# Two of 25 node groups take the sums of gathered rows of x over the edge blocks' own one-hots, instead of a count matrix

## The chip, the cores and the metric

One core of one Trainium2 chip runs the whole kernel. The metric is the device time of one execution in microseconds; the kernel before took 802.71 us (median of three runs, 802.51 to 804.0). TensorE is called PE, its weight loads PEld, VectorE DVE, ScalarE ACT, GpSimd POOL and SyncE SP.

## The reference

A graph layer over N = 6250 nodes and E = 206250 edges, sorted by `dst`, feature width 128, everything float32:

```
h = x @ W_node.T + b_node                  # [6250, 128]
e = edge_attr @ W_edge.T + b_edge          # [206250, 128]
msg = (h[src] + e) @ W_msg.T + b_msg
s = segment_sum(msg, dst, 6250);  deg = segment_sum(1, dst, 6250)
out = layernorm(x + s / max(deg, 1)[:, None])      # eps 1e-5, no scale or shift
```

All of it is linear before the norm. So the kernel needs, for each node, the sum of its edges' `edge_attr` rows and the sum of `x[src]` over its edges; both are multiplied by combined weights afterwards.

## The kernel before, in words

**Edge sums, by blocks.** The edges are cut into NS = 101 blocks of 2048 (16 tiles of 128 edges). A block's edges belong to some 64 neighbouring nodes. For each block SP loads the 1 MB of `edge_attr` into one of three slots of `edges` (`load_edges`); DVE makes 16 one-hots of 128 x 32 (`make_onehot`, L730) and one placing matrix (`make_place`, L736); PE sums the rows into four windows of 32 nodes (`sum_windows`, L547), ACT copies them (`copy_windows`, L1179), PE moves them to their place among 128 nodes (`place_windows`, L554) and DVE adds them into the column array `sums_e` at a column read from a register (`add_sums`, L746).

**Sums of x, by groups.** The nodes are cut into 25 groups of 250. A group takes one round. In it, for each pair of nodes, one window of 125 edge sources is fetched by an indirect DMA on POOL's queue (`load_window`, L479, three rounds ahead); DVE turns the sources into a block number and a row number (`make_keys`) and into one-hots of both (`make_hots`, L756: `row_hot` and `key_hot`, one pair of instructions for 25 windows, five pairs a round); PE multiplies them into counts (`count_fill`, L615, 125 matmuls a round, five to a fill, 25 fills a round), ACT moves each bank of counts to SBUF (`move_bank`, L1235), and in the next round PE multiplies all of x, split into three bfloat16 parts, with the counts (`apply_counts`, L630, 147 matmuls of 250 columns spread over the fills). The result, `x[src]` summed for 250 nodes, is copied to `group_x` (`take_x`), and `finish_group` (L641, L642) multiplies both sums with the weights; DVE and ACT make residual and norm, SP stores.

**Order.** The order is written out by hand, the same on every engine: 8 leading slots with one block each, then rounds of five slots s = 0 to 4, each slot of five fills. Edge blocks come in pairs, nearly always at the start of slots s = 2 and s = 4 of a round (`blocks_at`); the finish of an earlier group is in slot s = 0. PE works strictly in this order: it sums a slot's blocks, then does the fills; the blocks are placed after the slot's second fill. DVE makes the one-hots of slot g + 1 first in slot g, then does the adds of that slot's blocks. The blocks start at number 27 and wrap around, since the first 7 groups are done last. POOL's queue holds only the fetching of windows after some 110 us. SP's queue holds the edge loads in block order, with residual loads and stores between them.

If one of several checks on the inputs (sortedness, how far the edges of the groups reach) fails, a slow general path runs; every limit of those checks is met by these inputs with room, before and after the change.

## Time and profile before

| | before |
|---|---|
| median of 3 runs | 802.71 us |
| profiled execution, its own time | 799.62 us |
| span of its trace | 797.7 us |
| PE busy | 716.8 us (90%) |
| PEld busy | 649.6 us (81%) |
| DVE busy | 640.0 us (80%) |
| ACT busy | 467.9 us (59%) |
| POOL busy | 84.3 us (11%) |
| mean DMA rate | 152 GB/s |
| mean granted clock of PE | 0.987 of full speed |

The span is what the trace covers; the execution's own time is 1.9 us longer. Busy times are sums of the instructions' durations with overlaps counted once, so they tell how full an engine is, and the idle places have to be looked for in the slices, the chain and the timelines.

### The profile page before, as it was taken

The page shows a single profiled execution, that of the slowest core. Times are in us where ns is not written, and L with a number is a line of the kernel's source. Part 1 is how long each engine was busy: PE and PEld are TensorE (multiplying, and loading weights), DVE is VectorE, ACT ScalarE, POOL GpSimd, SP SyncE. Part 2 cuts the span into 40 slices and gives each one's busy share as a digit, 9 for nine tenths or more (in the row PEclk, how much of TensorE's full clock was granted, in tenths as well). Part 3 has the DMA queues.
Part 4 walks back from the last instruction along what each step waited for, and adds up shares of the span by engine and source line. Part 5 has one row for each costly group of instructions (what it writes and reads, how often), then busy time and mean ns, then how long its engine had stood idle before and what let it go on. Part 6 is the DMA issues. An engine that isn't in the chain of part 4 may idle for free.

```text
span 797.7 us, 24927 instructions
## 1 busy us (share of the span) xinstructions
PE 716.8 (90%) x10573; PEld 649.6 (81%) x10573; DVE 640.0 (80%) x1137; ACT 467.9 (59%) x948; POOL 84.3 (11%) x63
## 2 busy tenths in 40 slices
PE   2634458999999999999999999999999999999995
PEld 2523347899899999899999999998999999999995
DVE  7508998799988888888888888888888888888832
ACT  4103955576566666666666666566656666666641
POOL 2113734001000000000000000000000000000000
PEclk9999979999999999999999999999999999999999
DMA  6985334363365436243645463453345543644000
GB/s 209 209 268 176 106 108 128 108 229 123 130 207 173 169 118 236 59 170 119 228 135 182 144 227 125 155 186 117 123 149 187 186 160 118 221 150 174 31 14 16
DMA packets 71806, 121.11 MB, mean 152 GB/s; under 512 B 4717, under 2 KB 17738, under 8 KB 71591
## 3 DMA queue, kind: packets, MB, share of 16 engines
q1 hardware_dynamic: 68462, 115.72, 43.5%
q0 software_dynamic: 2496, 2.84, 1.5%
q8 instruction: 87, 1.43, 0.8%
q10 hardware_dynamic: 734, 0.90, 0.5%
q14 instruction: 27, 0.22, 0.1%
HBM read 116.19 MB, written 3.23 MB: 150 GB/s over the span
## 4 chain that ended last, share of the span: by engine, by line
PE 75%; DVE 14%; issue 4%; DMA 4%; SPq 2%; DVEq 1%; ACT 0%; ACTq 0%
PE x_ps L630 44%; PE count_ps L615 15%; PE win_ps L547 10%; DVE key_hot L756 3%; DVE row_hot L756 3%; PE win_ps L554 3%; DMA edges<-in_edge_attr_dram 2%; SPq L394 2%; DVE onehot L730 1%; PE misc_ps L641 1%; PE misc_ps L642 1%; DVE dve_junk L851 1%; DVE place L736 1%; DMA region<-in_dst_dram 1%; DMA rows_words<-starts_dram 1%
## 5 line engine op out<-in xcount | busy, mean ns | idle before, releaser
L1235 ACT CAST region<-count_ps 128x490 bf16<-128x490 f32 x625 | 354.1, 574 | 186.8 <-PE count_ps L615 182.2
L630 PE MATMUL x_ps<-region,x_rest 128*128 128x250 bf16 x2450 | 448.4, 269 | 0.0
L630 PE MATMUL x_ps<-region,x_hi 128*128 128x250 bf16 x1225 | 332.0, 271 | 0.5 <-ACT region L1235 0.5
L615 PE MATMUL count_ps<-key_hot,row_hot 125*128 125x98 bf16 x3125 | 242.4, 209 | 27.4 <-DVE key_hot L756 17.5
L756 DVE TENSOR_TENSOR row_hot<-iota_bf,row 125x3200 bf16<-125x3200 bf16 x125 | 229.8, 1838 | 34.2 <-PE count_ps L615 32.2
L630 PEld LDWEIGHTS x_ps<-region,x_rest 128*128 128x128 bf16 x2450 | 229.3, 98 | 17.2
L615 PEld LDWEIGHTS count_ps<-key_hot,row_hot 125*128 125x128 bf16 x3125 | 201.3, 98 | 50.0 <-DVE key_hot L756 20.6
L756 DVE TENSOR_TENSOR key_hot<-iota_bf,key 125x2500 bf16<-125x2500 bf16 x125 | 183.4, 1467 | 0.0
L547 PE MATMUL win_ps<-edges,onehot 128*32 128x128 f32 x3232 | 108.7, 290 | 18.7 <-DMA edges<-in_edge_attr_dram 16.9
L630 PEld LDWEIGHTS x_ps<-region,x_hi 128*128 128x128 bf16 x1225 | 118.7, 97 | 8.3 <-ACT region L1235 0.6
L547 PEld LDWEIGHTS win_ps<-edges,onehot 128*32 128x32 f32 x3232 | 91.4, 116 | 31.4 <-issue 29.8
L479 POOL DMA_INDIRECT win_src<-in_src_dram,clipped_int x25 | 47.8, 1910 | 528.1 <-DVE key_bf L785 406.6
L1179 ACT COPY win_sb<-win_ps 128x128 f32<-128x128 f32 x101 | 26.7, 267 | 95.2 <-PE win_ps L547 90.8
L746 DVE TENSOR_TENSOR sums_e<-sums_e,win_ps 128x128 f32 x101 | 29.1, 288 | 58.6 <-DVE sums_e L746 23.6
L730 DVE TENSOR_TENSOR onehot<-iota_bf,rel_col 128x512 f32<-128x512 bf16 x101 | 68.4, 715 | 0.0
L554 PE MATMUL win_ps<-place,win_sb 128*128 128x128 f32 x202 | 35.4, 297 | 6.4 <-DVE place L736 4.1
L554 PEld LDWEIGHTS win_ps<-place,win_sb 128*128 128x128 f32 x202 | 29.0, 204 | 9.2 <-ACT win_sb L1179 4.5
L736 DVE TENSOR_SCALAR place<-iota_f,pos 128x128 f32<-128x128 f32 x101 | 30.4, 339 | 0.0
L1253 ACT ACTIVATE y<-y,shift,rstd 125x128 f32<-125x128 f32 x50 | 21.9, 487 | 1.9 <-DVE shift L824 1.9
L795 DVE SCALAR_TENSOR_TENSOR y<-misc_ps,recip,resid 125x128 f32<-125x128 f32 x50 | 15.1, 344 | 8.9 <-PE misc_ps L642 8.9
L1242 ACT COPY group_x<-x_ps 128x250 f32<-128x250 f32 x25 | 9.2, 369 | 18.2 <-PE x_ps L630 16.5
L641 PE MATMUL misc_ps<-w_both,sums_e 128*125 128x128 f32 x100 | 19.2, 274 | 0.5 <-issue 0.5
(166 smaller groups left out, 341.9 us busy)
## 6 DMA issues: line engine op xcount, KB each, us to landing
edges<-in_edge_attr_dram SPq DMA_DIRECT2D x101, 1024.0 KB, 7.1
resid<-in_x_dram SPq DMA_DIRECT2D x25, 125.0 KB
out_dram<-y SPq DMA_DIRECT2D x25, 125.0 KB
region<-in_dst_dram ACTq DMA_DIRECT2D x1, 768.0 KB
win_src<-in_src_dram,clipped_int POOLq DMA_INDIRECT x25, 7.5
region<-in_L_gnn_W_node_dram SPq DMA_DIRECT2D x1, 64.0 KB
region<-in_L_gnn_W_edge_dram SPq DMA_DIRECT2D x1, 64.0 KB
region<-in_L_gnn_W_msg_dram SPq DMA_DIRECT2D x1, 64.0 KB
```

Of the source, the lines that this page charges most:

```text
L479: pool.indirect_dma_start(out=win_src[:, m % 3, :], out_offset=None, in_=src.rearrange("(r e) -> r e", e=WE), in_offset=bass.IndirectOffse ...
L547: mm = pe.matmul(bank[q * W:(q + 1) * W, 0:D], hot[:, q * J + j, :], edges[:, t % EDGE_SLOTS, q * J + j, :], start=(j == 0), stop=(j == J ...
L554: pe.matmul(l2_ps[t % 2], win_sb[:, t % 2, :], place[:, t % 2, :], start=True, stop=True).then_inc(l2_done, 1)
L615: mm = pe.matmul(count_ps[fill % COUNT_BANKS][:, k * KEYS:(k + 1) * KEYS], row_hot[0:WE, g % 2, f * FILL + k, :], key_hot[0:WE, g % 2, f * ...
L630: mm = pe.matmul(x_ps[m % 2][:, 0:NB], rows, counts[m % 2][:, b, :], start=(n == 0), stop=(n == PARTS - 1))
L641: pe.matmul(to, sums_e[:, first + h * PB:first + (h + 1) * PB], w_both[:, 1, :], start=True, stop=False)
L730: dve.tensor_tensor(onehot[:, t % ONEHOT_SLOTS, :, :], iota_bf[:, 0:W].rearrange("p (a w) -> p a w", a=1).to_broadcast([P, TILES, W]), rel ...
L736: dve.tensor_scalar(place[:, t % 2, :], iota_f[:, :], pos[:, sup_of[t]:sup_of[t] + 1], None, ALU.is_equal).then_inc(place_ready, 1)
L746: dve.tensor_tensor(to, to, l2_ps[t % 2], ALU.add).then_inc(added, 1)
L756: ins = dve.tensor_tensor(hot[0:WE, g % 2, :, :].rearrange("p w (a b) -> p w a b", b=4), iota_bf[0:WE, 0:width].rearrange("p (c a b) -> p ...
L1179: act.copy(win_sb[:, t % 2, :], win_ps[t % 2][:, 0:D]).then_inc(win_copied, 1)
L1235: act.copy(counts[m % 2][:, :, f * FILL * 2:(f + 1) * FILL * 2], count_ps[fill % COUNT_BANKS][:, 0:FILL * KEYS].rearrange("p (n b) -> p b ...
```

## The change

Groups 0 and 1 (nodes 0 to 499) no longer get a round: the rounds go from 25 to 23, and so do windows, keys, hots, counts and their application. For nine edge blocks (blocks 0 to 8, which cover nodes 0 to some 560) the rows `x[src]` are gathered from DRAM: 16 indirect DMAs of 128 rows of 512 B each on POOL's queue, into a new buffer `x_gathered` (one buffer, 1 MB in all). PE then runs `sum_windows` and `place_windows` a second time for that block, as a second *item*, with the same one-hots and the same placing matrix and `x_gathered` in the place of the edge rows; DVE adds the result into 700 other columns of `sums_e`, which ACT sets to zero before. `finish_group` takes the sum of x for groups 0 and 1 from there.

The nine blocks are taken in slot s = 3 of rounds 5, 6, 8, 10, 12, 13, 15, 17 and 19, a slot that had no block before: in it PE sums the edge rows first and the gathered rows next. The other 92 blocks keep the pairs in slots 2 and 4. The 16 gathers of a block are all asked for when PE has filled bank 25r - 7 of the counts (in slot 3 of the round before, r being the block's round), so 22 fills before slot 3 of round r. The first of them also waits until the block before has used `x_gathered`. The numbers of the sources come by nine direct DMAs on SP's queue (16 bytes a piece), early on. The two extra finishes lie in slot 3 of rounds 14 and 20.

```diff
+GX = 2
+XBLOCKS = 9
-    ROUNDS = GROUPS
+    ROUNDS = GROUPS - GX
...
+    XSEG = 3
+    x_round = [5 + 14 * k // (XBLOCKS - 1) for k in range(XBLOCKS)]
+    x_slot = [LEAD + SEGS * m + XSEG for m in x_round]
...
+    x_fill = []
+    for k in range(XBLOCKS):
+        room = (x_round[k] - x_round[k - 1] if k > 0 else 2) * ROUND_FILLS
+        x_fill.append([x_round[k] * ROUND_FILLS + XSEG * FILLS - room + 2 + (room - 24) for i in range(TILES)])
+    pool_loads = sorted([(ROUND_FILLS * (m - 3) + 10, 0, m) for m in range(2, ROUNDS)] + [(x_fill[k][i], 1, k * TILES + i) for k in range(XBLOCKS) for i in range(TILES)])
...
+                if LEAD <= t < LEAD + XBLOCKS:
+                    k = t - LEAD
+                    with nc.allow_non_contiguous_dma(reason="four sources a piece"):
+                        sp.dma_start(x_index[:, k, :].rearrange("p (q j) -> p q j", q=Q),
+                                     src[k * SUP:(k + 1) * SUP].rearrange("(q p j) -> p q j", q=Q, j=J)).then_inc(x_index_in, 16)
...
-            for m in range(2, ROUNDS):
-                load_window(m)
+            def load_rows(k, i):
+                if i == 0:
+                    pool.wait_ge(x_index_in, 16 * XBLOCKS)
+                    pool.wait_ge(src_index_ready, 3)
+                    if k > 0:
+                        pool.wait_ge(l1_done, last_item[sup_of.index(k - 1)] + 1)
+                pool.wait_ge(bank_filled, x_fill[k][i])
+                pass_waits()
+                pool.indirect_dma_start(out=x_gathered[:, i, :], out_offset=None, in_=x[:, :],
+                                        in_offset=bass.IndirectOffsetOnAxis(ap=x_index[:, k, i:i + 1], axis=0)).then_inc(rows_in, 16)
+
+            for fill, kind, at in pool_loads:
+                if kind == 0:
+                    load_window(at)
+                else:
+                    load_rows(at // TILES, at % TILES)
...
-            def sum_windows(t):
-                hot, bank = onehot[:, t % ONEHOT_SLOTS, :, :], win_ps[t % 2]
+            def sum_windows(v):
+                t, k = item_of[v]
+                hot, bank = onehot[:, t % ONEHOT_SLOTS, :, :], win_ps[v % 2]
                 pe.wait_ge(onehot_ready, t + 1)
...
-                pe.wait_ge(edge_in[t % EDGE_SLOTS], 16 * (t // EDGE_SLOTS + 1))
+                if k is None:
+                    pe.wait_ge(edge_in[t % EDGE_SLOTS], 16 * (t // EDGE_SLOTS + 1))
+                else:
+                    pe.wait_ge(rows_in, 16 * TILES * (k + 1))
...
+                        rows = edges[:, t % EDGE_SLOTS, q * J + j, :] if k is None else x_gathered[:, q * J + j, :]
...
+                if u == ZERO_X:
+                    act.wait_ge(fin_mm, ZERO_FIN)
+                    act.copy(sums_e[:, X_COLS:X_COLS + X_LONG], zero_col[:, 0:1].to_broadcast([P, X_LONG])).then_inc(zeroed, 1)
```

On DVE three small instructions are new ahead of the rounds (`base_x`, `limit_x` and a check). The scratch of the early node counting moves into `x_gathered`.

## Rows read from the trace of the kernel before

**Rows 1.** The page, part 1: busy us of each engine, its share, instructions.
```profile
PE 716.8 (90%) x10573; PEld 649.6 (81%) x10573; DVE 640.0 (80%) x1137; ACT 467.9 (59%) x948; POOL 84.3 (11%) x63
```

**Rows 2.** The chain in order of time: start us, us, what (two of its pairs).
```profile
431.38 1.88 PE win_ps L547 x64
...
458.61 1.88 PE win_ps L547 x64
```

**Rows 3.** PE's timeline: start us, us, engine, line, operation, count.
```profile
438.00 0.38 PE L615 MATMUL count_ps<-key_hot,row_hot 125*128 125x98 bf16 x5
...
439.62 0.39 PE L615 MATMUL count_ps<-key_hot,row_hot 125*128 125x98 bf16 x5
...
445.95 0.52 PEld L554 LDWEIGHTS win_ps<-place,win_sb 128*128 128x128 f32 x4
...
446.39 0.35 PEld L615 LDWEIGHTS count_ps<-key_hot,row_hot 125*128 125x128 bf16 x5
...
452.36 0.29 PEld L641 LDWEIGHTS misc_ps<-w_both,sums_e 128*125 128x125 f32 x2
...
453.24 0.34 PEld L615 LDWEIGHTS count_ps<-key_hot,row_hot 125*128 125x128 bf16 x5
```

**Rows 4.** POOL's timeline: the indirect DMAs of L479, five of 25.
```profile
57.43 1.21 POOL L479 DMA_INDIRECT win_src<-in_src_dram,clipped_int  x1 [27.56 <-DVEq L881]
58.95 1.21 POOL L479 DMA_INDIRECT win_src<-in_src_dram,clipped_int  x1 [0.30 <-issue]
...
124.43 2.82 POOL L479 DMA_INDIRECT win_src<-in_src_dram,clipped_int  x1 [0.30 <-issue]
127.56 2.80 POOL L479 DMA_INDIRECT win_src<-in_src_dram,clipped_int  x1 [0.30 <-issue]
...
433.91 1.90 POOL L479 DMA_INDIRECT win_src<-in_src_dram,clipped_int  x1 [25.34 <-DVE key_bf L785]
```

**Rows 5.** DVE's timeline beside two of these.
```profile
124.35 1.83 DVE L756 TENSOR_TENSOR row_hot<-iota_bf,row 125x3200 bf16<-125x3200 bf16 x1
...
432.91 1.82 DVE L756 TENSOR_TENSOR row_hot<-iota_bf,row 125x3200 bf16<-125x3200 bf16 x1
```

**Rows 6.** DVE's timeline over one round, its long instructions that matter.
```profile
439.64 1.82 DVE L756 TENSOR_TENSOR row_hot<-iota_bf,row 125x3200 bf16<-125x3200 bf16 x1
...
442.75 1.82 DVE L756 TENSOR_TENSOR row_hot<-iota_bf,row 125x3200 bf16<-125x3200 bf16 x1
...
448.01 1.28 DVE L730 TENSOR_TENSOR onehot<-iota_bf,rel_col 128x512 f32<-128x512 bf16 x2
449.22 1.82 DVE L756 TENSOR_TENSOR row_hot<-iota_bf,row 125x3200 bf16<-125x3200 bf16 x1
...
453.77 1.83 DVE L756 TENSOR_TENSOR row_hot<-iota_bf,row 125x3200 bf16<-125x3200 bf16 x1 [1.36 <-PE count_ps L615]
...
460.14 1.82 DVE L756 TENSOR_TENSOR row_hot<-iota_bf,row 125x3200 bf16<-125x3200 bf16 x1
...
465.70 1.29 DVE L730 TENSOR_TENSOR onehot<-iota_bf,rel_col 128x512 f32<-128x512 bf16 x2
466.91 1.82 DVE L756 TENSOR_TENSOR row_hot<-iota_bf,row 125x3200 bf16<-125x3200 bf16 x1
```

**Rows 7.** The answer on line 479: time from issue to landing of its DMAs.
```profile
DMA to landing us min/median/max: 3.3/7.5/9.3
```

**Rows 8.** The page, part 6: KB each, median us from issue to landing.
```profile
edges<-in_edge_attr_dram SPq DMA_DIRECT2D x101, 1024.0 KB, 7.1
```

**Rows 9.** Stretches: length, PE, PEld, DVE, ACT, POOL busy, granted clock, DMA.
```profile
400.00:500.00 100.00, 100.00 (x1567) 91.61 (x1565) 86.81 (x144) 64.15 (x130) 7.59 (x4) 1.00 0.49 163
...
130.00:140.00 10.00, 6.85 (x78) 6.09 (x76) 8.11 (x22) 3.33 (x6) 2.26 (x2) 0.92 0.59 203
140.00:150.00 10.00, 9.59 (x149) 8.12 (x148) 6.61 (x13) 5.67 (x12) 0.00 (x0) 0.91 0.46 144
```

**Rows 10.** The chain in order of time around that stretch.
```profile
132.46 5.02 DMA rows_words<-starts_dram
```

More of the change, by code:

```diff
@@ L95, in gnn_layer @@
-    summed_by = [blocks_by[u] for u in finish_slot]
-    assert not any(blocks_at[u] for u in finish_at)
-    LIMIT_B = (39.5, 3.7)
-    LIMIT_A = (6.0, 3.7)
-    for m, done in enumerate(summed_by):
-        if m < B_ROUNDS:
-            assert LIMIT_B[0] + LIMIT_B[1] * m <= FIRST + done or FIRST + done >= NS, m
-        else:
-            assert done == NS or LIMIT_A[0] + LIMIT_A[1] * (m - B_ROUNDS) <= FIRST + done - NS, m
+        due = u + 1 if u < LEAD else min(NS - XBLOCKS, LEAD + 2 * pairs)
@@ new lines, in gnn_layer @@
+        blocks_at.append(list(range(len(sup_of), len(sup_of) + due - ordered_by[-1])))
+        sup_of += ordered[ordered_by[-1]:due]
+        item_of += [(t, None) for t in blocks_at[u]]
+        ordered_by.append(due)
+        if u in x_slot:
+            assert not blocks_at[u]
+            k = x_slot.index(u)
+            blocks_at[u].append(len(sup_of))
+            item_of += [(len(sup_of), None), (len(sup_of), k)]
+            sup_of.append(k)
+        items_by.append(len(item_of))
+    ITEMS = len(item_of)
@@ new lines, in gnn_layer @@
+    finishes = [(LEAD + SEGS * (m + 2) if m < ROUNDS - 2 else SLOTS, m, None) for m in range(ROUNDS)]
+    for i in range(GX):
+        u = x_slot[X_DONE[i] - 1] + SEGS
+        finishes.append((u if u not in x_slot else u + SEGS, None, i))
+    finishes.sort(key=lambda f: f[0])
+    finish_slot = [f[0] for f in finishes]
+    finish_of = {m: n for n, (u, m, i) in enumerate(finishes) if m is not None}
+    finished = [i if m is None else group_of[m] for u, m, i in finishes]
+    finish_at = {u: n for n, u in enumerate(finish_slot) if u < SLOTS}
@@ new lines, in gnn_layer @@
+    assert not any(blocks_at[u] for u in finish_at) and len(finish_at) == GROUPS - 2
+    ZERO_FIN = 1 + max(n for n, g in enumerate(finished) if g * NB < X_COLS + X_LONG and (g + 1) * NB > X_COLS)
+    ZERO_X = finish_slot[ZERO_FIN - 1] + 1
+    assert ZERO_X < x_slot[0] and X_COLS >= N0 + P and (GX - 1) * NB + 322 + P <= X_LONG
+    LIMIT_B = (39.5, 3.7)
+    LIMIT_A = (5.3, 4.0)
+    LIMIT_X = (3.0, 2.0)
+    for u, m, i in finishes:
+        done = FIRST + ordered_by[u]
+        if m is None:
+            assert LIMIT_X[0] + LIMIT_X[1] * (2 * i + 1) <= X_DONE[i]
+        elif m < B_ROUNDS:
+            assert LIMIT_B[0] + LIMIT_B[1] * m <= done or done >= NS, m
+        else:
+            assert done == NS + FIRST - XBLOCKS or LIMIT_A[0] + LIMIT_A[1] * group_of[m] <= done - NS + XBLOCKS, (m, done)
@@ L159, in gnn_layer @@
         before_hot = [words.rearrange("p (j n) -> p j n", j=TILES) for words in before_words]
[L160 to L161 removed]
+        act_junk = [spare[:, k * JUNK:(k + 1) * JUNK].bitcast(BF16) for k in range(2)]
+        dve_junk = [spare[:, (2 + k) * JUNK:(3 + k) * JUNK].bitcast(BF16) for k in range(2)]
         is_last = sb("is_last", [P, 1])
@@ L634, in finish_group @@
             def finish_group(n):
-                first = group_of[n] * NB
-                pe.wait_ge(added, summed_by[n])
-                pe.wait_ge(x_taken, n + 1)
+                u, m, i = finishes[n]
+                first = finished[n] * NB
+                pe.wait_ge(added, items_by[u])
+                if m is not None:
+                    pe.wait_ge(x_taken, m + 1)
+                    x_sums = group_x[:, m % 2, :]
+                else:
+                    x_sums = sums_e[:, X_COLS + i * NB:X_COLS + (i + 1) * NB]
                 free_misc()
```

137 lines of the change are left out of this document (78 added, 59 removed).

## The prediction

> **What bounds the kernel now.** Read first the engines' shares: PE is busy for 90% of the span and DVE for 80%, POOL for 11% [rows 1]. Then the stretches: between 400 and 500 us PE is busy for 100.00 of 100 us at full clock, DVE for 86.81 [rows 9]. So in the steady part PE's own instruction stream sets the pace, DVE has 13 us in 100 to spare, and what PE does not have to execute is gained in full, as long as nothing makes it wait. The chain shows the period: the block pair of slot 2 starts at 431.38 in one round and at 458.61 in the next [rows 2], so a round takes 27.23 us.
>
> **What is removed.** A pair of blocks costs PE 1.88 us for the sums [rows 2] and 446.39 - 445.95 = 0.44 us for the placing [rows 3], together 2.32. A finish costs 453.24 - 452.36 = 0.88 us [rows 3]. Both are done as often as before (101 blocks, 25 finishes), only in fewer rounds. What a round costs beyond them is 27.23 - 2 x 2.32 - 0.88 = 21.71 us, and two such rounds go: **-43.4 us**. DVE loses two rounds of one-hots too, so it does not become the bound: it keeps about its share.
>
> **What is added on PE.** Nine more items at half a pair's price: 9 x 1.16 = **+10.4 us**, if the rows are there. The half pairs in slot 3 make one slot as full as the pair slots around it; DVE prepares one block's one-hots for it instead of two's, so I take nothing for it.
>
> **Whether the gathered rows are there.** This decides the case. One round of before serves as the clock. The slot s = 3 begins with the fill at 438.00, its third fill is at 439.62 and over at about 440.0 [rows 3]; that is bank 25r - 7, at which POOL may begin. The rows are needed one round after the slot's start, at 438.00 + 27.23 = 465.23, plus 0.94 for the edge item that goes first: 466.17. The budget is 26.2 us for 16 gathers and the landing of the last.
>
> What a gather costs is not in the trace, but its nearest row is close: the window fetch, the same instruction with 125 rows of 500 B for 128 of 512 B. Alone it takes 1.21 us, and the next begins 58.95 - 57.43 = 1.52 after it [rows 4]. Beside DVE it is longer: 2.82 us where it began just after a `row_hot` (124.43 after 124.35), and the next one began 3.13 later and took 2.80. At 433.91 it took 1.90 and ended at 435.81; the `row_hot` beside it ran from 432.91 to 434.73 [rows 4, 5]. Both cases fit one rule: a gather that begins under a `row_hot` ends 1.08 us after the `row_hot` does (434.73 + 1.08 = 435.81; 124.35 + 1.83 + 1.08 = 127.26, seen 127.25). The `key_hot` that follows at once didn't hold it. I take that each gather needs a moment, about 0.1 us after its start, in which no `row_hot`, `key_hot` or `onehot` runs, and 1.09 us from there, with 0.30 between two.
>
> By this I walk through the round [rows 6], with the ends of `row_hot` at 441.46, 444.57, 451.04, 455.60 and 461.96. The gathers end at 442.6, 445.7, 447.2, 448.7, 450.4 (behind the `onehot` that ends at 449.29), 452.1, 453.6, 456.7, 458.2, 459.8, 463.1, 464.6 and 466.1. Thirteen are out when PE arrives. By then DVE has one more pair of hots in hand (466.91 to 470.1), after which it stops, as its adds need PE. The last three end at 468.1, 469.8 and 471.3. The last one starts at 470.1, and no edge load is under way by then, so I add the least landing time of 3.3 [rows 7]: 473.4, a stall of 7.2 us. With one gather more slipped in between two instructions it is 5.7. I take **7.0 us, nine times: +63.0**. Least: no hold by DVE at all, 440.1 + 15 x 1.52 + 3.3 = 466.2, a stall of 0.0. Most: the last lands at the median of 7.5 instead of 3.3 and one more gather is held for a `row_hot`, 7.2 + 4.2 + 1.6 = 13. PE is the bound and all five slots of a round are full, so nothing makes the stall good later. Behind PE's waiting instruction stand the placing, the fills and the counts of x; DVE waits in its adds for the placing, ACT for banks. In round 17 the pair of slot 2 is missing, which makes the budget 2.3 shorter; that is within the 7.0's error.
>
> The Trainium skill speaks of this place: *SBUF — State Buffer*, section "Who interferes with whom", has the port pair that DVE and GpSimd share as an exclusive lock, but lets `tensor_tensor` take only its read interface and infers that descriptor generation, which writes, isn't held up by it. By that rule the gathers would run at the pace of the undisturbed ones and the stall would vanish. The trace doesn't agree: beside a TENSOR_TENSOR the same instruction took 1.90 and 2.82 instead of 1.21 us.
>
> **The clock after a stall.** Once before, PE stood for 5.02 us on a DMA (132.46) [rows 10]. The granted clock is 0.92 in the stretch 130 to 140 and 0.91 in 140 to 150 [rows 9], with PE at work again from 137.5. A fall from 2.4 to 1.2 GHz counts half, so that is 10 x 0.17 x 2 = 3.4 us at the lower level, 1.7 us lost. A stall of 7 us should cost the same each time: 9 x 1.7 = **+15.3 us**. Least 0, most twice that.
>
> **Small parts.** Three small instructions on DVE before the rounds, where the chain runs through DVE: +0.5 us at a guess, bounds 0 and 1. The zeroing of 700 columns is ACT's, which is 59% busy [rows 1]: 0. The nine index loads go through SP's queue ahead of edge loads; an edge load takes 7.1 us to land [rows 8] and is asked for three blocks ahead, so one moved by some 1 to 2 us is still in time: 0, at most 9 x 1 = 9 if the early part has no such cover. The gathers move 9 x 1 MB more over DMA engines that were half used (0.49 in the steady stretch [rows 9]): 0.
>
> **The sum.** 797.7 - 43.4 + 10.4 + 63.0 + 15.3 + 0.5 = 843.5 us of span. The profiled execution's own time is 1.9 above its span (799.62), and the median of the runs is 3.1 above that: **848.5, say 848 us**, 5.7% slower. The likeliest case's own range is 825 to 880: stalls of 5.7 to 9.5 us with 0 to 2.5 for the clock.
>
> **The rivals.**
> *The gathers are in time* (the side of faster). Mechanism: POOL's instruction gets its moment at every change of instruction on DVE, or the source of the hold is something that gathers with ready indices don't need. Then stall and clock cost are gone: 797.7 - 43.4 + 10.4 + 0.5 + 5.0 = 770 us. For it: 1.21 us and a period of 1.52 undisturbed; the sum fits the budget to 0.0. Against: all steady fetches took 1.90. The point from which it decides is (43.4 - 10.4 - 0.5) / 9 = 3.6 us per block, clock included. Chance 0.14. By the rule of the Trainium skill weighed above (*SBUF — State Buffer*, "Who interferes with whom") this is what happens.
> *A short stall*, 0.5 to 3.5 us per block and hardly a fall of the clock: 775 to 801, at its middle 788. For it: DVE's pattern beside new slots may leave more room than in my walk. Chance 0.08.
> *A long stall.* The landing is at the median or worse since the gathers share the engines with edge loads asked for at the same time, and a `key_hot` holds a gather too: 13 us and 2.5 of clock per block, 770 + 9 x 15.5 = 909; half way to it 880 to 900. For it: 7.5 is the median landing time. Against: during the stall hardly an edge load is asked for. Chance 0.12.
> *The change doesn't do what it says*: an input check fails and the general path runs, at many times 800 us. The limits and the node counts leave room; chance under 0.01.
>
> The main case has 0.65. The range for 8 in 10 takes in the short stall's upper part and most of the long one: 782 to 888. A difference under 0.2% (1.6 us) can't be told from none here: faster 0.22, the same 0.01, slower 0.77.
>
> **What would show it.** In the changed trace: a period of 27.2 us in rounds without a gathered block; nine waits of PE's `win_ps` for a DMA into `x_gathered`, 5 to 9 us each, and these rounds at 27.2 + 1.2 + 7 + 1.7 = 37 us; POOL's gathers at 1.2, 1.9 and 2.8 us by where they start, some 13 before PE arrives; the granted clock under 1.00 behind each wait. The prediction is wrong if the waits are under 3.6 us, and the mechanism is wrong if the gathers' durations don't go with DVE's `row_hot`.

## The result and the profile after

| | before | after |
|---|---|---|
| median, four runs each on the same chip | 802.61 us | 926.87 us |
| ratio, with its interval | | 1.1547 (1.151 to 1.1584) |
| span of the trace | 797.7 us | 925.6 us |
| mean granted clock of PE | 0.987 | 0.906 |

The change costs 15.5% where 5.7% was forecast; the time lies above the range's 888. All medians below are of runs beside a kernel before on the same chip, which took 800.2 to 802.6 us; each kernel was run twice, but e3 ten times, e9 five, e13 and e17 four. The ratios are of fast executions: one of e13's four, with 2423.57 us, and one of the kernel before beside it, with 875.22, are left out, and no trace shows what slowed them.

The page after, part 1 and PE's share and clock in 40 slices; the first line answers to [rows 1]:

```profile
PE 749.2 (81%) x10331; PEld 641.0 (69%) x10331; DVE 609.9 (66%) x1120; ACT 438.7 (47%) x902; POOL 249.0 (27%) x205
...
PE   3444489999896997997895978993998897799996
...
POOL 2123620011826027008207061035008208100000
```

PE executes 242 matmuls fewer than before in 128 us more. Its share falls in single slices, most of them slices in which POOL's digit is high. The stretch that answers to [rows 9] (us, then busy us and number of instructions of each engine, PE's clock, DMA share, GB/s) has PE busy for 85.44 us where it was 100.00:

```profile
400.00:500.00 100.00, 85.44 (x1173) 70.97 (x1171) 64.17 (x104) 46.27 (x94) 36.73 (x29) 0.89 0.41 133
```

The forecast wanted nine waits of PE for a DMA into `x_gathered`. The trace has none. This is the answer on the tile `x_gathered` for PE after (288 matmuls form the 144 of x's second items twice over, since a float32 matmul is shown as two); under "idle before it" stands nothing:

```profile
L622 PE MATMUL win_ps<-x_gathered,onehot x288: 272/273/273, 267.8 to 805.4; 128*32 128x128 f32 x144
its engine sat idle before it (us, times) until:
who waited for it (us, times):
```

Besides waits for PE itself, what stands long in the waits after is "issue", an engine that waited for nothing that the trace shows, and "remote", an event without a known sender (engine, tile and line, what ended the idle time, us in total, times, longest):

```profile
ACT region L1327 <- remote: 87.8, 23, 10.8
DVE row_hot L841 <- remote: 86.1, 8, 15.7
...
PEld win_ps L622 <- issue: 57.5, 87, 17.6
PEld x_ps L705 <- issue: 49.1, 42, 14.6
```

So the lost time begins at PE. POOL's timeline shows the first burst (start us, us, engine, line, operation, idle before); it answers to [rows 4]:

```profile
228.26 5.87 POOL L565 DMA_INDIRECT x_gathered<-in_x_dram,x_index  x1 [32.10 <-PE count_ps L690]
234.44 0.95 POOL L565 DMA_INDIRECT x_gathered<-in_x_dram,x_index  x1 [0.30 <-PE count_ps L690]
...
237.22 2.03 POOL L565 DMA_INDIRECT x_gathered<-in_x_dram,x_index  x1 [0.30 <-issue]
239.56 1.06 POOL L565 DMA_INDIRECT x_gathered<-in_x_dram,x_index  x1 [0.30 <-issue]
...
243.43 1.60 POOL L565 DMA_INDIRECT x_gathered<-in_x_dram,x_index  x1 [0.30 <-issue]
...
246.70 0.94 POOL L565 DMA_INDIRECT x_gathered<-in_x_dram,x_index  x1 [0.30 <-issue]
247.95 0.94 POOL L565 DMA_INDIRECT x_gathered<-in_x_dram,x_index  x1 [0.30 <-issue]
...
254.19 0.94 POOL L565 DMA_INDIRECT x_gathered<-in_x_dram,x_index  x1 [0.30 <-issue]
```

And PE in the same time, in three stretches:

```profile
236.00:246.00 10.00, 9.24 (x111) 8.26 (x108) 7.42 (x8) 5.31 (x10) 8.17 (x7) 1.00 0.43 149
247.00:258.00 11.00, 6.16 (x26) 1.81 (x26) 1.74 (x10) 1.14 (x2) 7.52 (x8) 0.62 0.21 52
259.00:266.00 7.00, 7.00 (x86) 5.99 (x79) 4.09 (x9) 2.97 (x8) 0.00 (x0) 0.69 0.54 170
```

In the middle stretch PE executes 26 matmuls in 11 us, 2.4 a us, against 11 before it and 12 behind it. Its timeline there (the sums of an ordinary pair of edge blocks, whose rows and one-hots are long there) has small groups with gaps between them:

```profile
247.20 0.86 PE L622 MATMUL win_ps<-edges,onehot 128*32 128x128 f32 x4
248.39 0.38 PE L622 MATMUL win_ps<-edges,onehot 128*32 128x128 f32 x3 [0.33 <-issue]
249.83 0.44 PE L622 MATMUL win_ps<-edges,onehot 128*32 128x128 f32 x2 [1.06 <-issue]
250.56 0.37 PE L622 MATMUL win_ps<-edges,onehot 128*32 128x128 f32 x1 [0.29 <-issue]
```

I call this crawling. It begins while gathers go out back to back, lasts until some 3 us after the last one's instruction (over at 255.13 in this block, PE back at its rate at 258.5), and occurs in all nine blocks, in pair sums as here or in the fills. The clock follows: 1.00 in the first stretch, 0.62 in the second, where the trace has 2.4 GHz until 249.7 and 1.2 GHz for the 13.7 us from there. Of stretches of 2 us, 72 after 200 us hold fewer than 24 instructions of PE (matmuls and weight loads) where 50 are usual; before, none does until its last 10 us. They hold 675 instructions, worth 27 us at 50 to 2 us, so 144 - 27 = 117 us are lost in them.

The other engines also hear from PE late, and this makes "issue" and "remote" less empty than they look. ACT moves one bank of counts for each fill, in order, so its n-th cast belongs to the n-th fill. In the seventh block two fills end at 624.75 and 625.61, and their banks are moved at 632.05 and 641.23, though ACT had nothing else to do:

```profile
624.36 0.39 PE L690 MATMUL count_ps<-key_hot,row_hot 125*128 125x98 bf16 x5
...
625.22 0.39 PE L690 MATMUL count_ps<-key_hot,row_hot 125*128 125x98 bf16 x5
...
632.05 0.57 ACT L1327 CAST region<-count_ps 128x490 bf16<-128x490 f32 x1 [5.18 <-remote]
641.23 0.57 ACT L1327 CAST region<-count_ps 128x490 bf16<-128x490 f32 x1 [8.60 <-remote]
...
641.86 0.39 PE L705 MATMUL x_ps<-region,x_hi 128*128 128x250 bf16 x1 [13.94 <-issue]
```

The trace's record of the semaphore that PE counts up for the second of these fills stands at 641.21, 15.6 us after the fill. PE's next instruction needs all banks of its round moved and starts 0.06 us after the cast is over, so these 13.94 us of "issue" are a wait for ACT, which itself waited for PE's late word (540 records of ACT's own semaphore are in the trace for 575 casts, against 574 in e1's). Counted over the fills after 200 us, ACT starts more than 0.5 us behind both the fill and its own work before in 49 of 481 cases, up to 10.8 us and 125.6 us in all; in the kernel before it never starts more than 0.04 us behind.

The length of the rounds says where (us between ACT's copies of the row numbers, one a round, worked out from the traces; after, and e1, which is after without gathers):

```
after  35.8 38.5 30.6 27.5 28.8 43.9 43.0 27.2 45.5 27.2 44.9 25.4 51.7 51.3 27.2 50.4 27.2 42.7 27.2 45.8 27.2 29.5
e1     35.8 38.6 28.8 27.5 28.9 30.9 28.3 27.2 30.8 27.2 30.8 25.4 30.8 30.8 27.2 33.0 27.2 27.2 27.2 30.8 27.2 29.5
```

Rounds of the steady part without gathers take 27.2 us, as [rows 2] has it; rounds in which a block is gathered take 13 to 21 us more than the same rounds of e1.

### The profile page after: what moved, and what is told of

It is laid out like the page before. It is cut to its first block, busy times and chain, and to the rows that moved or that the text cites. A ratio compares the mean times of both kernels' runs of the same rounds, so it can differ in the third digit from the quotient of the medians.

```text
span 925.6 us, 24735 instructions
## 1 busy us (share of the span) xinstructions
PE 749.2 (81%) x10331; PEld 641.0 (69%) x10331; DVE 609.9 (66%) x1120; ACT 438.7 (47%) x902; POOL 249.0 (27%) x205
## 4 chain that ended last, share of the span: by engine, by line
PE 59%; DVE 16%; issue 11%; another core or an unknown queue 6%; DMA 3%; SPq 1%; ACT 1%; DVEq 1%; ACTq 0%
PE x_ps L705 32%; PE count_ps L690 12%; PE win_ps L622 11%; DVE key_hot L841 4%; DVE row_hot L841 4%; PE win_ps L629 2%; DMA edges<-in_edge_attr_dram 2%; DVE onehot L811 1%; SPq L444 1%; PE misc_ps L721 1%; PE misc_ps L722 1%; DVE x_gathered L936 1%; DVEq L822 1%; ACT region L1327 1%
## 5 line engine op out<-in xcount | busy, mean ns | idle before, releaser
L1327 ACT CAST region<-count_ps 128x490 bf16<-128x490 f32 x575 | 323.4, 574 | 294.8 <-PE count_ps L690 200.5
L705 PE MATMUL x_ps<-region,x_rest 128*128 128x250 bf16 x2254 | 434.6, 278 | 12.7 <-issue 12.3
L705 PE MATMUL x_ps<-region,x_hi 128*128 128x250 bf16 x1127 | 315.5, 280 | 25.5 <-issue 22.1
L841 DVE TENSOR_TENSOR row_hot<-iota_bf,row 125x3200 bf16<-125x3200 bf16 x115 | 211.6, 1840 | 131.5 <-remote 86.1
L565 POOL DMA_INDIRECT x_gathered<-in_x_dram,x_index x144 | 177.3, 1231 | 344.2 <-PE count_ps L690 306.1
L690 PEld LDWEIGHTS count_ps<-key_hot,row_hot 125*128 125x128 bf16 x2875 | 190.7, 101 | 83.6 <-issue 38.3
L705 PEld LDWEIGHTS x_ps<-region,x_rest 128*128 128x128 bf16 x2254 | 216.9, 101 | 40.8 <-issue 21.5
L841 DVE TENSOR_TENSOR key_hot<-iota_bf,key 125x2500 bf16<-125x2500 bf16 x115 | 168.6, 1466 | 0.0
L622 PE MATMUL win_ps<-edges,onehot 128*32 128x128 f32 x3232 | 128.9, 298 | 39.8 <-DMA edges<-in_edge_attr_dram 17.3
L534 POOL DMA_INDIRECT win_src<-in_src_dram,clipped_int x23 | 35.3, 1535 | 156.1 <-issue 77.6
L629 PEld LDWEIGHTS win_ps<-place,win_sb 128*128 128x128 f32 x220 | 32.2, 206 | 19.6 <-issue 13.7
```

The lines of the kernel that those rows point to most:

```text
L534: pool.indirect_dma_start(out=win_src[:, m % 3, :], out_offset=None, in_=src.rearrange("(r e) -> r e", e=WE), in_offset=bass.IndirectOffse ...
L565: pool.indirect_dma_start(out=x_gathered[:, i, :], out_offset=None, in_=x[:, :], in_offset=bass.IndirectOffsetOnAxis(ap=x_index[:, k, i:i ...
L622: mm = pe.matmul(bank[q * W:(q + 1) * W, 0:D], hot[:, q * J + j, :], rows, start=(j == 0), stop=(j == J - 1))
L629: pe.matmul(l2_ps[v % 2], win_sb[:, v % 2, :], place[:, t % 2, :], start=True, stop=True).then_inc(l2_done, 1)
L690: mm = pe.matmul(count_ps[fill % COUNT_BANKS][:, k * KEYS:(k + 1) * KEYS], row_hot[0:WE, g % 2, f * FILL + k, :], key_hot[0:WE, g % 2, f * ...
L705: mm = pe.matmul(x_ps[m % 2][:, 0:NB], rows, counts[m % 2][:, b, :], start=(n == 0), stop=(n == PARTS - 1))
```

## The experiments

All kernels are the changed kernel with the edit shown. The first question: is the loss in a wait for the rows, in the gathers themselves, or in the rest?

**e1, no gathers.**

```diff
-                pool.wait_ge(bank_filled, x_fill[k][i])
-                pass_waits()
-                pool.indirect_dma_start(out=x_gathered[:, i, :], ...).then_inc(rows_in, 16)
+                if k == 0 and i == 0:
+                    pool.memset(x_gathered[:, :, :], 0.0).then_inc(rows_in, 16)
```

> The 144 gathers are left out; POOL sets the buffer to zero once, and PE doesn't wait for rows. It leaves out the sums of x for groups 0 and 1. Everything else of the change stays: 23 rounds, nine second items, index loads. Both theories: the terms -43.4 and +10.4 of my sum hold, and the time is 770 us (765 to 776), all of the loss belongs to the gathers. If it is over 790, the loss lies in the new order of blocks or in the second items.

Measured: 780.1 us, ratio 0.9751 (0.9724 to 0.9779). Everything but the gathers is a gain, if a smaller one than my 32.5 us of span: 797.7 - 779.6 = 18.1. A part of the missing 14.4 is a wait that I had priced at nothing, PE for DVE's one-hots in the slot behind the extra one:

```profile
PE win_ps L618 <- DVE onehot L807: 8.4, 8, 1.1
```

Of the other 6 us, 2.4 lie ahead of the first copy of row numbers (68.7 us against 66.3) and 1.6 behind the last (59.6 against 58.0); the rest is not located. The gathers cost 926.9 - 780.1 = 147 us, 16.3 a block.

**e2, the same bursts, and nothing waits for them.** The second items sum edge rows again, and POOL alone keeps count of the gathers; the output for 500 nodes is thus other than the reference's.

```diff
-                    sp.wait_ge(l1_done, first_item[t - EDGE_SLOTS] + 1)
+                    sp.wait_ge(l1_done, last_item[t - EDGE_SLOTS] + 1)
...
+                        pool.wait_ge(rows_in, 16 * TILES * k)
...
-                    pe.wait_ge(rows_in, 16 * TILES * (k + 1))
+                    pe.wait_ge(edge_in[t % EDGE_SLOTS], 16 * (t // EDGE_SLOTS + 1))
```

> All gathers run as in the changed kernel, in the same bursts, but the second items sum the edge rows again, so that nothing waits for the gathered rows; it leaves out the sums of x for groups 0 and 1. Theory A (the burst itself slows PE's instructions, whoever waits for it): as slow as the changed kernel, 927 us (915 to 935), PE at some 5 instructions per us in the bursts. Rival W (PE is late because its rows land late, and the slow matmuls are how the trace shows this wait): 770 us (765 to 780).

Measured: 924.6 us, 1.1558 (1.1521 to 1.1595), as with the waits. The wait that my forecast was built on is worth nothing here; PE crawls all the same.

**e3, gathers spread.** One every 2 to 3 fills instead of all at once.

```diff
-        x_fill.append([x_round[k] * ROUND_FILLS + XSEG * FILLS - room + 2 + (room - 24) for i in range(TILES)])
+        x_fill.append([x_round[k] * ROUND_FILLS + XSEG * FILLS - room + 2 + i * (room - 5) // TILES for i in range(TILES)])
```

> The 16 gathers of a block are spread evenly over all fills since the block before (45 of 50 fills for seven blocks, one gather in 2.8 fills, 20 of 25 fills for two blocks, one in 1.25 fills). Theory A, with a backlog that builds up only when gathers follow each other at 1.25 us: seven blocks lose nothing, two lose some; 770 + 2 x 0 to 17 us, that is 770 to 805, likeliest 785. If the damage goes with the number of gathers and not with their rate: 927 as before. Rival W: rows are asked for earlier, 770 to 780.

Measured: 802.8 us, 1.0031 (1.0015 to 1.0048), all of the output computed. The same 144 gathers, and 124 of the 147 us are gone. What is left is mostly in the two blocks that have only one round between them and the block before, whose 16 gathers stand 1.25 fills apart: 37.6 and 39.7 us instead of 28.3 and 30.8 of e1, together 18 of 23 us.

**e4, a quarter of the bytes, and e5, a quarter of the rows.** Both fill only a part of the buffer, which is zero elsewhere.

```diff
-                pool.indirect_dma_start(out=x_gathered[:, i, :], out_offset=None, in_=x[:, :],
+                pool.indirect_dma_start(out=x_gathered[:, i, 0:32], out_offset=None, in_=x.rearrange("n (h e) -> (n h) e", e=32),
```

```diff
-                pool.indirect_dma_start(out=x_gathered[:, i, :], out_offset=None, in_=x[:, :],
-                                        in_offset=bass.IndirectOffsetOnAxis(ap=x_index[:, k, i:i + 1], axis=0)).then_inc(rows_in, 16)
+                pool.indirect_dma_start(out=x_gathered[0:32, i, :], out_offset=None, in_=x[:, :],
+                                        in_offset=bass.IndirectOffsetOnAxis(ap=x_index[0:32, k, i:i + 1], axis=0)).then_inc(rows_in, 16)
```

> As the changed kernel in number and time of the gathers, but each fetches 128 pieces of 128 B instead of 128 rows of 512 B (wrong rows, the rest of the buffer zero). Theory A by descriptors, semaphore writes or POOL's generation: 927 us stays (over 900). Theory A by bytes moved: under 810 us. Rival W: somewhat faster landing, 880 to 927.

> As the changed kernel, 16 gathers in a burst per block, but each fetches 32 rows instead of 128 (the rest of the buffer stays zero, so the sums of x for groups 0 and 1 lack three quarters of their rows). Descriptors and bytes go to a quarter, the number of DMAs and of their completions stays. Theory A1 (the number of descriptors, or POOL's time on them): the slow stretches vanish, 780 to 795 us. Theory A2 (the completions, one per DMA engine and gather): 900 us or more stays, as the burst even gets denser.

Measured: 921.2 us (1.1515, 1.149 to 1.154) and 936.5 us (1.168, 1.157 to 1.179). Fewer bytes or fewer rows make it no better. Most gathers of 32 rows took 0.87 us, those of 128 rows 0.94: what an indirect DMA costs on POOL is nearly all fixed.

**e6 and e7, other paces.** Groups of four gathers every 11 fills (5 in the two narrow blocks), and one gather every 1.5 fills (1.25 there).

```diff
+        ... - room + 2 + i // 4 * (5 if room == 25 else 11) for i in range(TILES)])     # e6
+        ... - room + (2 + i * 20 // TILES if room == 25 else 20 + i * 3 // 2) for i in range(TILES)])     # e7
```

> Gathers in groups of four back to back, a group every 11 fills (seven blocks) or every 5 fills (two blocks, the mean rate of the two dense blocks in the run with even spreading). If it takes a backlog of six or more gathers at 1.25 us to slow PE: no slow stretch in the seven blocks, and hardly one in the two: 785 to 795 us. If every gather that follows another at 1.25 us costs: 840 us or more.

> In seven blocks a gather every 1.5 fills (1.6 us) instead of every 2.8; the two dense blocks at 1.25 fills as with even spreading, where they cost some 9 us each. If the limit lies between 1.25 and 1.5 us a gather: 800 to 806 us, like even spreading. If at 1.6 us the backlog builds up too: 830 to 870.

Measured: 828.0 us, 1.0327 (1.025 to 1.040), and 818.6 us, 1.021 (1.013 to 1.029). The wide rounds lose some 0.5 to 5 us each; single gathers, though closer together on average than the groups, cost less than groups of four.

**e8, the same pieces by SP.** 16 direct DMAs of 128 rows by SP's hardware queue in place of POOL's, of rows in their natural order (so the sums of x for 500 nodes are of other rows, as in e10, e11 and e15).

```diff
+                while asked < XBLOCKS and slot_of[t] >= x_slot[asked] - 4:
...
+                    for i in range(TILES):
+                        sp.dma_start(x_gathered[:, i, :], x[i * P:(i + 1) * P, :]).then_inc(rows_in, 16)
```

> No gathers; SP asks for 16 direct DMAs of 128 rows of 512 B each per block, in a run, some four slots ahead: same number of DMAs, of 512 B pieces, of bytes and of completions into the same semaphore, but by SP's hardware queue (rows 0 to 2047 of x each time, so the sums of x for groups 0 and 1 are wrong ones). If any such burst slows PE: over 850 us. If it takes POOL's software-made descriptors: 780 to 800 us, less 0 to 10 of edge loads that come later.

Measured: 790.5 us, 0.9859 (0.9815 to 0.9904). No crawling; 10 us above e1, of which one round took 41.9 instead of 30.8 for an edge load that came late behind them. The landing of 9 MB more, its writes to SBUF and its semaphore updates are thus harmless to PE's stream, and the fault is with POOL's part.

The second question: what about POOL's instruction is it?

**e10 and e11, direct DMAs by POOL,** 16 of 128 rows or one of 2048:

```diff
-                pool.indirect_dma_start(...)
+                pool.dma_start(x_gathered[:, i, :], x[i * P:(i + 1) * P, :]).then_inc(rows_in, 16)     # e10
+                pool.dma_start(x_gathered[:, :, :], x[0:TILES * P, :].rearrange("(i p) d -> p i d", p=P)).then_inc(rows_in, 16)     # e11, i == 0 only
```

> The changed kernel with each indirect gather replaced by a plain direct DMA of POOL, of 128 rows of 512 B with known addresses (the sums of x for 500 nodes are then of other rows), 16 in a burst at the same place, the same bytes and the same completion. If it is the indirection (reading the indices, one descriptor a row computed from them) that slows PE, this stands with the gathers left out or with SP's sixteen direct DMAs: 780 to 795. If it is any burst of DMAs whose descriptors POOL makes, PE crawls here too: 900 to 930. Between them if direct descriptors are made in less time.

> As the sixteen direct DMAs of POOL, with one direct DMA of 2048 rows of 512 B in their place; rows are thus other ones again. If the number of POOL's DMA instructions decides: 780 to 790. If the descriptors it makes decide: as the sixteen direct ones. If direct ones of POOL are harmless altogether, both stand at 780 to 795 and the fault is with the indirect form.

Measured: 779.4 us, 0.9729 (0.9695 to 0.9763), and 777.2 us, 0.9701 (0.9669 to 0.9733). Harmless; but 16 of them are through in some 9 us, which is shorter than the 19 us after which PE began to crawl in the first block (in the fifth and sixth, on the sums of a pair, 3 us were enough, and e10 shows nothing there either). **e15** makes the stretch as long, with 48 direct ones of 48, 48 and 32 rows, and **e16** keeps POOL busy as long without any DMA (16 memsets of the buffer; the sums of x of 500 nodes are zero):

```diff
+                for a, b in ((0, 48), (48, 96), (96, 128)):
+                    pool.dma_start(x_gathered[a:b, i, :], x[i * P + a:i * P + b, :]).then_inc(rows_in, 16)     # e15
+                if k * TILES + i > 0:
+                    pool.wait_ge(rows_in, 16 * (k * TILES + i))
+                pool.memset(x_gathered[:, :, :], 0.0).then_inc(rows_in, 16)     # e16
```

> As the sixteen direct DMAs of POOL (e10, 779.4 us, a burst of some 8.7 us), with 48 direct ones of 48, 48 and 32 rows in their place, some 0.55 us each, so a burst of about 25 us, as long as that of the 16 gathers (rows of known addresses, so other sums of x for 500 nodes). If the length of an unbroken stretch of POOL's DMA issue decides, PE crawls here too: 880 to 930. If it is the indirect form: 780 to 785.

> The changed kernel with each gather replaced by POOL's memset of the whole buffer of gathered rows (1.8 us each, 16 in a burst of some 30 us, no DMA); the sums of x for 500 nodes are zero. If it takes DMAs to slow PE's instructions: 780 to 790, the last of a burst may be 5 us late for PE (then 9 waits more, up to 830, and they show as waits of PE for POOL). If POOL being busy without a pause is enough: PE's rate falls from 25 to about 5 instructions a us 10 us into the burst, and over 880.

Measured: 821.7 us (1.0264, 1.022 to 1.031) and 842.3 us (1.0522, 1.049 to 1.056). By time alone both look like the fault. The waits say otherwise; PE's for e15, then for e16:

```profile
PE win_ps L622 <- DMA x_gathered<-in_x_dram: 26.4, 9, 7.5
```

```profile
PE win_ps L623 <- DVE onehot L812: 23.9, 8, 3.4
PE win_ps L623 <- POOL x_gathered L567: 22.9, 8, 7.4
```

Here PE does wait for the buffer, as the bursts (24 us of direct DMAs at 0.50 a piece, 31 us of memsets) are too long for the time they have, and in e16 for DVE's one-hots, 23.9 us against 8.4 in e1; ahead of the waits it runs at its full rate. Ten us in the middle of a burst of e16 have 129 matmuls:

```profile
235.00:245.00 10.00, 10.00 (x129) 9.18 (x131) 8.80 (x13) 7.07 (x13) 9.38 (x6) 1.00 0.22 85
```

and as many of e15, of its burst from 261.63 to 285.44:

```profile
265.00:275.00 10.00, 10.00 (x128) 9.38 (x126) 7.64 (x6) 6.25 (x13) 10.00 (x21) 1.00 0.19 47
```

So neither POOL at work without a pause nor its direct DMAs do it: it takes the **indirect** ones. The late word from PE to ACT goes the same way: fills that ACT takes up more than 0.5 us late are found in all runs above whose indirect gathers lost time (52 in e2, 46 in e4, 42 in e5, 35 in e6, 39 in e7, 15 in e3), and not one in e1, e8, e10, e11, e15 and e16. And e15 is by chance the case that I had forecast: nine waits of 2.9 us on average, 26.4 in all, and 821.7 - 780.1 = 41.6 us lost, so 15.2 for other things, the clock above all: after 200 us it stands at 1.2 GHz for 39.6 us against 9.1 in e1, and 30.5 us at half speed cost 15.2.

The third question: how many in a row?

**e12 and e14, the first 8 or 12 gathers of each burst** (the rest of the buffer zero), and **e13 and e17, all 16 in two bursts of 8**, 11 fills apart in the changed kernel's slots or 17 apart in those of e9:

```diff
+                if i >= 8:      # e12; 12 in e14
+                    return
...
+        ... + (room - 24) + 11 * (i // 8) for i in range(TILES)])     # e13
+        x_fill.append([(x_slot[k] - LEAD) * FILLS - room + 2 + 17 * (i // 8) for i in range(TILES)])     # e17
```

> The changed kernel with only the first 8 of the 16 gathers of each block, back to back at the same place; the other 1024 rows of the buffer stay at the zeros written once, so the sums of x for 500 nodes are those of half of their edges. In the trace PE crawls only from 5 to 10 us after the burst began. If the loss has such an onset (something fills up and then blocks), half a burst costs much less than half: under 3 us a block, 785 to 810. If each gather costs the same, half of 926.9 - 780.1 = 147 is lost: 853. In groups of four a block lost 828 - 780 = 48 over 9 = 5.3 us, which speaks for something between, some 820.

> The changed kernel with only the first 12 of the 16 gathers of a block, back to back; 512 rows of the buffer stay zero, so the sums of x for 500 nodes lack a quarter of their edges. If the loss begins after 8 and then costs the same for each gather more, half of 926.9 - 780.1 is lost with 12: about 853. If it begins after 12 (15 us): 780 to 790. If 8 and 16 stand on either side of a sudden step, the value shows where.

> The changed kernel with the 16 gathers of a block in two bursts of 8, the second 11 fills after the first; slots and everything else as in the changed kernel. One burst of 8 cost nothing (779.3 us, e12, against 780.1 without gathers). If the loss begins only after some 8 gathers without a pause: 780, but in a block that has to wait for the buffer (the two with one round between) both bursts fall together and cost 10 to 15 us each: 795 to 810. If the sum of gathers within a round decides, it loses as the groups of four did or more: 830 to 925.

> The kernel with even gaps (e9) with the 16 gathers of a block in two bursts of 8, the second 17 fills (18.5 us) after the first, in place of one gather every 2 to 3 fills. A burst of 8 lasts 12 us, or 17 where the first gather takes 5.8, so there are 1.5 to 6 us of pause. If the loss belongs to an unbroken stretch of more than 8 gathers: 775 to 785, as e9. If a pause of a few us doesn't reset it: some 850 as the burst of 12, or up to 890.

Measured: 779.3 us with 8 (0.9728, 0.9695 to 0.976), 854.1 us with 12 (1.067, 1.063 to 1.071), 885.6 us (881.7 to 888.4) with two bursts of 8 (1.1081, 1.104 to 1.112), 869.7 us with two and a longer distance (1.0848, 1.077 to 1.092). Eight cost nothing, twelve half of the loss: it looks like an onset, then a price for each further gather. But e13 was ill chosen (in five of its nine blocks the second burst follows the first after 0.3 us), and e17, where there were pauses, shows that 8 is no safe number. In it PE begins to crawl already in the third gather where that falls on the sums of a pair, in four places in the second. The stretches of e17 around one such place, where the gathers start at 314.53, 315.79, 317.11 and 318.56 and PE's loads falter from 317.7:

```profile
312.00:316.00 4.00, 4.00 (x62) 3.58 (x55) 2.49 (x7) 2.07 (x5) 1.16 (x2) 1.00 0.73 245
318.00:321.00 3.00, 1.23 (x10) 0.57 (x10) 2.93 (x6) 0.76 (x2) 2.39 (x3) 1.00 0.19 45
328.00:334.00 6.00, 6.00 (x44) 4.94 (x43) 1.90 (x6) 2.21 (x5) 0.00 (x0) 0.58 0.94 349
```

The same holds in e6, where seven crawls begin in the third gather of a group, each after 43 to 45 instructions of a pair's sums. In the fills, where PE executes 25 instructions a us instead of 60 to 75, crawling begins between the fifth gather (278.0 us in the changed kernel's second block) and the tenth (its first block).

Nor is the number in a row the whole rule. In the fifth block of e12 and of e14 the first gathers start alike (427.17, 428.65, 429.92 and 443.06, 444.54, 445.80), and the sums of a pair start 1.47 us behind the first. Two us of each from there, e12 first:

```profile
428.60:430.60 2.00, 2.00 (x68) 1.76 (x67) 1.80 (x2) 0.90 (x3) 1.64 (x2) 1.00 0.25 66
```

```profile
444.50:446.50 2.00, 1.69 (x38) 1.17 (x37) 1.82 (x2) 0.63 (x2) 1.66 (x2) 1.00 0.27 66
```

e12 runs at its full rate with two gathers under way, and e14 crawls after 34 weight loads. In e12 no fill at all is taken up late; in e14 36 are, and in its first block one is 0.50 us late already in the third gather (233.6 us), where e12 has 0.04. So that 8 are harmless is a finding of e12 and not of any burst of 8, and what makes the two differ before their ninth gather is not known.

**e9, even gaps,** the version that the spread pointed to: slots for the nine blocks at least seven apart, and the 16 gathers of a block spread evenly over the stretch since the block before. **e18** has e9's slots with the burst.

```diff
-    x_round = [5 + 14 * k // (XBLOCKS - 1) for k in range(XBLOCKS)]
-    x_slot = [LEAD + SEGS * m + XSEG for m in x_round]
+    x_slot = [LEAD + g for g in (28, 36, 46, 53, 63, 71, 81, 88, 98)]
...
-        room = (x_round[k] - x_round[k - 1] if k > 0 else 2) * ROUND_FILLS
-        x_fill.append([x_round[k] * ROUND_FILLS + XSEG * FILLS - room + 2 + (room - 24) for i in range(TILES)])
+        room = (x_slot[k] - x_slot[k - 1] if k > 0 else 2 * SEGS) * FILLS
+        x_fill.append([(x_slot[k] - LEAD) * FILLS - room + 2 + i * (room - 5) // TILES for i in range(TILES)])     # e9
+        x_fill.append([(x_slot[k] - LEAD) * FILLS - 22 for i in range(TILES)])     # e18
```

> The changed kernel with the nine gathered blocks in slots 28, 36, 46, 53, 63, 71, 81, 88 and 98 after the leading ones, so that at least seven slots (35 fills) lie between two of them, and with the 16 gathers of a block spread evenly over that stretch (2 to 3 fills apart). If the loss goes by the rate of the gathers, as the spread and the groups of four suggest (about 1.1 us a block at 2.8 fills, 2.8 at 1.5 fills, and twice as much in the two blocks that had only 50 - 5 fills beside a full slot), this comes to 780.1 + 9 x 1.1 = 790, and it is faster than the kernel before by some 1.5%. If each gather costs PE the same wherever it stands, it comes out like the first spread, 803. Rounds in which the extra block falls beside a pair may cost 2 to 5 us in all on top: DVE's one-hots are late there.

> The slots of e9 with the burst of 16 gathers of the changed kernel, asked for 22 fills before the block's slot. If the pace of the gathers is the whole matter, it loses as the changed kernel does, less the 5 us by which e9's slots are better than the others (775.4 against 780.1 without gathers): about 920. If the slots matter, because the burst falls beside other work of DVE and the blocks no longer follow each other in the next round but one: 800 to 890.

Measured: e9 **775.4 us, 0.968 (0.9658 to 0.9702)**, all of the output computed: 3.2% faster than the kernel before and 4.7 us under e1; PE waits 4.4 us for one-hots in e9's slots against 8.4 in e1's (these slots without gathers were not run). No fill is taken up late. e18 927.5 us, 1.1586 (1.152 to 1.165): the slots are worth nothing against the burst. Between the two lies nothing but when POOL may ask for a gather. A part of POOL's timeline in e9, then its page's first line and PE's row:

```profile
317.60 0.94 POOL L563 DMA_INDIRECT x_gathered<-in_x_dram,x_index  x1 [0.88 <-PE count_ps L688]
320.20 1.61 POOL L563 DMA_INDIRECT x_gathered<-in_x_dram,x_index  x1 [1.66 <-PE count_ps L688]
322.69 0.94 POOL L563 DMA_INDIRECT x_gathered<-in_x_dram,x_index  x1 [0.89 <-PE count_ps L688]
326.18 1.51 POOL L563 DMA_INDIRECT x_gathered<-in_x_dram,x_index  x1 [2.54 <-PE count_ps L688]
```

```profile
PE 686.2 (89%) x10331; PEld 618.8 (80%) x10331; DVE 610.2 (79%) x1120; ACT 440.1 (57%) x902; POOL 270.7 (35%) x205
...
PE   2624549899999999999999999999999999999995
```

POOL is busier than after (270.7 against 249.0 us), and PE's row has its nines back.

## Why the prediction was wrong, point by point

**The rounds removed and the items added** (-43.4 + 10.4): right in sign, too good by 14.4 us. Nothing was taken for DVE in the full slots, and the slots behind them have PE wait 8.4 us in all for one-hots (e1). A round with a gathered block holds the edge item too, which the forecast's 27.2 + 1.2 had left out: 27.2 + 2 x 1.16 = 29.5, and most of e1's take 30.8.

**The pace of the gathers**: the shape was right, its constants were too dear. A gather that begins under a `row_hot` ends a fixed time behind it in 13 of 19 cases: 237.22 + 2.03 = 239.25 for a `row_hot` over at 238.44, and 245.03 for 244.21, so 0.81 to 0.83 us where the walk had 1.08. Undisturbed it takes 0.94 instead of 1.21, with a period of 1.25. Both are 0.27 less, so it is one constant that the window fetch has higher than a gather. Five of the other six are first gathers of a burst, which end 5.31 or 5.32 us behind the `row_hot`; the walk had no such case. Nor had all steady fetches of the kernel before taken 1.90 us: one took 2.82 (190.03) and one 1.53 (272.72). That rule of mine even feeds the fault: when PE crawls, DVE has less to do and holds no gather, so the rest of the burst goes out at 1.25 us each.

**The wait of PE at the second item, nine times 7.0, +63.0: this step failed.** There is no such wait (none in the trace; e2 is not faster without it). Of the range's two ends, 0.0 and 13, the least one holds, in a kernel that loses 16.3 us a block, and by luck: from the start of the first gather to the end of the last 25.4 to 27.1 us pass in five of the nine blocks, with the landing still to come, where the budget was 26.2 us with it. By this PE would have had to wait there, had it not been later itself.

**The term that was missing** is in the small parts: the gathers' cost to the other engines was counted as bytes, at 0, and the bytes are indeed harmless (e4, e8). What costs is that POOL's indirect DMAs, one after another, slow PE's instruction stream to a quarter and less and hold back its word to the others. It is the whole difference of 147 us, of which 117 lie in the crawling stretches; the other 30 (work at 1.2 GHz behind a crawl, shorter crawls) I have not taken apart. No row of the kernel before shows two indirect DMAs back to back in its steady part, so the trace could not have told it; what could be seen was that the change puts POOL into a state of which the trace has no example, and that deserved a bound in both directions rather than a zero.

**The clock**, 1.7 us behind each wait: right where there is a wait. In e15 the loss beyond the 26.4 us of waits is 15.2 us over nine blocks, 1.7 each. In the changed kernel the clock stands at 1.2 GHz for 155.8 us after 200 us, a part of it while PE crawls, where it follows from the crawling.

**The rivals.** *The gathers are in time* forecast 770, near e9's 775.4, where the gathers are asked for one by one and earlier; its account, that DVE doesn't hold them, is not borne out. *A long stall*, 880 to 909, is nearest to 926.9 in number, and there is no stall. The Trainium skill, page *SBUF — State Buffer*, section "Who interferes with whom", infers that a `tensor_tensor` does not hold up the generation of descriptors. That does not agree here (2.03 us beside `row_hot`, 0.94 without). The same section of the Trainium skill states "DMA never contends with a compute engine". That agrees as far as landing data goes (e8, 790.5 us), but the making of these DMAs on POOL does reach another compute engine (926.9 against 780.1 us). Its advice to move a DMA to a hardware queue is for one that DVE stalls, which no run here puts to the test; in e8 it was PE's crawling that went away, for pieces of known addresses.

**What stays open** is what POOL's indirect DMA and PE share, such that PE's instructions and its counting up of semaphores are both held back. It isn't the landing, the bytes, the completions, the number of rows, POOL's being busy, or its direct DMAs. Not told apart are the indirect form and the scattered addresses of its rows: no run gathers rows in their natural order by indices. PE's instruction code comes in by DMA too, in 85 packets of 16 KB; in the crawls these packets still come at the same instructions of PE as in e12, within 80 (40 matmuls and their loads), and not at the ends of crawls (260 us in the first block, 280.7 in the middle of the second), so lack of code is not seen at this grain. That a crawl sets in sooner where PE executes more instructions a us speaks for something that PE draws on by the instruction. This is argued, not shown.

## What to carry to other kernels

Ask for indirect gathers one at a time with pauses (here 2.5 us from start to start in the median, 1.25 to 7.3 at the ends; the kernel then gained 3.2% where the burst of the same gathers lost 15.5%), even if the buffer would allow all of them at once, and keep them off the stretches in which TensorE executes many short instructions (this from where the crawls of e6 and e17 begin; no run tested it alone). When a trace shows an engine slow with "issue" or no releaser in front of its instructions, look at what runs on the other engines from the moment the rate falls, and take that away or spread it; and compare the end of each producer with the start of its consumer, since a record that is missing hides a wait. And price an operation that the trace holds only singly as unknown for the others when the change issues it in a row.

## What the hardware showed that I had not expected

- PE's rate falls from about 11 matmuls a us to 2.4 during back-to-back indirect DMAs of POOL; from the second or third in pair sums, from the fifth to tenth in the fills. Once it starts nothing for 14.1 us (627.7 to 641.9).
- ACT takes up a finished fill up to 10.8 us late during such bursts, and 0.04 us behind it in the kernel before.
- An indirect DMA of 32 rows costs POOL 0.87 us and one of 128 rows 0.94; a direct one of 48 or 32 rows 0.51, one of 128 rows 0.54, one of 2048 rows 1.22.
- The first gather behind some 30 us or more of rest took 5.80 to 6.27 us in five of nine bursts (5.87 at 228.26); the cause was not looked into.
